# State-space stage: the load of the log/exp table moves from behind the sines to behind the square of B

## The chip, the cores and the metric

One Trainium2 chip, one of its cores. The metric is device time in microseconds (us) of one execution of the whole program; the figure for a kernel is the median of several runs. The engines are TensorE (PE in the profile, its weight loads PEld), VectorE (DVE), ScalarE (ACT), GpSimd (POOL) and SyncE (SP, which issues DMA here).

## The reference

Two layers over x of shape 8 x 512 x 256, float32: causal attention and a sparse SwiGLU, then a selective state space and a mixture of experts. Each is added to its input behind a layer norm. The change is in the state space, of which this is the core (64 heads of 8 channels, state size N = 128):

```python
Bm = (x @ WB.T).reshape(B_, L, H, N)
Cm = (x @ WC.T).reshape(B_, L, H, N)
Bm = rmsnorm(Bm, Bn_w) + B_bias      # x * rsqrt(mean(x*x) + EPS) * w
Cm = rmsnorm(Cm, Cn_w) + C_bias
theta_cumsum = jnp.cumsum(theta * dt[..., None], axis=1)
Bm = rope(Bm, theta_cumsum)          # cos and sin of the summed angles
Cm = rope(Cm, theta_cumsum)
alpha = jnp.exp(dt * A)
h = at * h + bt * outer(B_prev, x_prev) + gt * outer(Bt, xt)   # for each t
yt = einsum(Ct, h)
```

## The kernel before

The program is a row of stages with a barrier behind each. In `state_space` the 64 heads are taken as 32 pairs, and a pair with one of the 8 sequences is a unit: 256 units, one turn of the loop each. The loop is written out for two turns (`j` = 0 and 1) and each engine has its own copy of it, in an order fixed by hand; an engine takes its instructions strictly in that order, and engines meet by semaphores that count turns. There is one buffer of most things, so the engines run as a pipeline over neighbouring turns rather than over copies of a buffer.

TensorE, turn k (`turn`): odd half of B (into `p_b`, waits for the rotation before), angles of the next unit into `p_sum` (waits for `ln_c`), outputs of the unit before the last, even half of B and `b_done`, the exponents of the decays (`e_done`), odd half of C, transposes of the unit before (L1246, L1249: `turned[0]`), the sum of the squares of B over partitions (L1280, waits for GpSimd's `ss_b` and for VectorE's `fr_done`), even half of C (waits for `taken[0]`), more transposes, scores (L1261), chunk sums (L1270), and the sum of the squares of C (L1280 again, waits for GpSimd's `ss_c`). Each projection is six matmuls, lines L48 to L50.

ScalarE, turn k: square of B (L1359, waits for `b_done`, releases GpSimd), exponential of the decays (L1339), a copy that empties the transposes' bank (L1345, `taken[0]`), logarithm and exponential of B's sum (L1350, L1352: together the inverse root), a second copy (L1345), square of C (L1365), logarithm and exponential of C's sum, and then `angles`: Abs (L1330), three sines (L1331, L1332, L1334) of the next unit's angles. Sines need another table than logarithm and exponential, so twice a turn a table is loaded: the sine table, placed by the compiler ahead of the first sine (it stands at L1331), and the log/exp table, asked for at L1335 as the last instruction of `angles`, ahead of the next turn's square.

GpSimd, turn k: adds the two halves of the squares of B (L1159, waits for `sq_b`), finishes C's rotation of the unit before (L1143, L1144), splits a piece of the next pair's weights (L1163, L1165), adds to the decays (L1149, L1150), adds the halves of the squares of C (L1171), scales x (L1180, L1182), finishes B's rotation (L1186, L1187), and builds `own` (L1192).

VectorE, turn k: the phases of the next-but-one angles (`phases`: L1392, the scan L1394, L1396, L1397, which ends with `fr_done`), L1401 and L1402 for the output, normalizing and rotating B (L1409, L1412, L1414, waits for ScalarE's `r_b`), the states (L1419 to L1423), the masked scores (L1428), and normalizing and rotating C (the same lines, waits for `r_c`).

Of the kernel before, what the change touches and what calls it, by code (L numbers as in the profile page):

```python
# [967 lines left out]
def state_space(nc, ctx, w_dram, norm_d, bias_d, left_d, right_d, strict_d, blocks_d, heads_d, tk_dram, dt_dram,  # L968
# [15 lines left out]
    with ExitStack() as mem:  # L984
# [337 lines left out]
        @block.scalar  # L1322
        def _(act):
            A = nc.scalar.activation
            act.wait_ge(const_in, 16 * 7)
            act.wait_ge(const_ready, at_start)

            def angles(count, j):
                act.wait_ge(fr_done, count)
                A(trig[:, j, 1], fr[:], ACT.Abs).then_inc(abs_done, 1)  # L1330
                A(trig[:, j, 0], fr[:], ACT.Sin, scale=UNDER_TURN)  # L1331
                A(trig[:, j, 2], fr[:], ACT.Sin, scale=-UNDER_TURN)  # L1332
                act.wait_ge(abs_done, count)
                A(trig[:, j, 1], trig[:, j, 1], ACT.Sin, bias=quarter[:, 0:1], scale=-UNDER_TURN).then_inc(trig_done, 1)  # L1334
                nc.scalar.preload_act_table_set("natural_log_exp_and_others")  # L1335

            def decays(k):
                act.wait_ge(e_done, k + 1)
                A(dec[:], p_se[:], ACT.Exp).then_inc(d_done, 1)  # L1339

            def take_b(k, j, e):
                act.wait_ge(turned[e], k + 1)
                n = TPB - e
                bank = p_m[:] if e else p_c[:, 0, :]
                A(bt[:, 2 if e else j, 0:n, :], bank[:, 0:n * P].rearrange("p (c t) -> p c t", t=P), ACT.Copy).then_inc(taken[e], 1)  # L1345

            def norms(k, q):
                done, ln, ready = (sum_b, sum_c)[q], (ln_b, ln_c)[q], (r_b, r_c)[q]
                act.wait_ge(done, k + 1)
                A(r[:, q], p_sum[:], ACT.Ln, scale=1.0 / N1, bias=eps[:, 0:1]).then_inc(ln, 1)  # L1350
                act.wait_ge(ln, k + 1)
                A(r[:, q], r[:, q], ACT.Exp, scale=-0.5).then_inc(ready, 1)  # L1352

            angles(1, 0)
            with act.Fori(0, UNITS // 2) as n:
                for j in range(2):
                    k = n * 2 + j
                    act.wait_ge(b_done, k + 1)
                    A(sq[:, 0], p_b[:], ACT.Square).then_inc(sq_b, 1)  # L1359
                    decays(k)  # L1360
                    take_b(k, j, 0)
                    norms(k, 0)
                    take_b(k, j, 1)
                    act.wait_ge(c_done, k + 1)
                    A(sq[:, 1], p_c[:], ACT.Square).then_inc(sq_c, 1)  # L1365
                    norms(k, 1)
                    angles(k + 2, 1 - j)
            decays(UNITS)
            take_b(UNITS, 0, 0)
            take_b(UNITS, 0, 1)  # L1370
# [508 lines left out]
```

## Time and profile before

| | us |
|---|---|
| median of 3 runs | 7745.34 |
| lowest, highest | 7743.88, 7745.35 |
| the profiled execution | 7747.07 |
| its span, first to last instruction | 7745.3 |
| state-space stage in it (2623 to 6985) | 4362 |

The span runs from the first to the last instruction of one profiled execution; its own time is that span and the little that lies around it. In the rows below a time is us from the span's start. A timeline row gives the start, the duration, engine, line, operation, what is written and read, and in brackets how long the engine had been idle and who ended that. PEclk in a view by stretches is TensorE's granted clock as a share of full speed.

### The profile page before, as it was taken

The numbers are of one execution on the slowest core, as the hardware profiler recorded it, in microseconds if no ns is written. First come the engines' busy times: TensorE is split into PE (matmuls) and PEld (weight loads), VectorE is DVE, ScalarE is ACT, GpSimd is POOL, SyncE is SP. The second block draws the span as 40 slices with busy tenths as digits, with TensorE's granted clock in tenths as the row PEclk, the third lists the DMA queues.
The fourth block names the chain that finished last, engine by engine and source line by source line (L and its number), as shares of the span: only waits on it lengthen the run. The fifth ranks groups of instructions, "written<-read, shape, count | busy, mean of one in ns | idle before, by whom it ended". The sixth has DMA issues, their size and how long they took to land. (4 is left out here: it accounts for less than half of the span.)

```text
span 7745.3 us, 137299 instructions
## 1 busy us (share of the span) xinstructions
PE 6985.7 (90%) x43387; PEld 5087.3 (66%) x43660; DVE 4741.5 (61%) x8121; ACT 3713.1 (48%) x5855; POOL 3482.4 (45%) x3893
## 2 busy tenths in 40 slices
PE   6999999999684699999999999999999999997499
PEld 4777777777573566666666666666666666666287
DVE  4333333333555477777777777777777777772433
ACT  2222222222222366666666666666666666662111
POOL 0000000000000477777777777777777777771000
PEclk8555555555796899999999999999999999998699
DMA  1000000000101211111111111111111111112100
GB/s 47 4 9 1 4 9 4 9 4 1 57 22 49 89 27 29 28 27 27 28 29 27 30 27 27 29 27 30 27 28 27 27 29 29 29 27 95 53 22 16
DMA packets 388293, 214.26 MB, mean 28 GB/s; under 512 B 248036, under 2 KB 343076, under 8 KB 387140
## 3 DMA queue, kind: packets, MB, share of 16 engines
q1 hardware_dynamic: 379588, 203.05, 10.1%
q10 hardware_dynamic: 8448, 8.39, 0.3%
q8 instruction: 88, 1.44, 0.1%
q14 instruction: 169, 1.38, 0.1%
HBM read 162.02 MB, written 40.64 MB: 26 GB/s over the span
## 5 line engine op out<-in xcount | busy, mean ns | idle before, releaser
L1117 POOL MEMSET ss_rot<- 128x4096 f32 x1 | 3.5, 3511 | 2500.9 <-POOLq L1815 2500.9
L1350 ACT ACTIVATE ss_r<-ss_pssum,ss_eps 128x512 f32<-128x512 f32 x512 | 352.5, 688 | 1131.1 <-PE ss_pssum L1280 1131.1
L1280 PE MATMUL ss_pssum<-ss_sq,ss_pairssum 128*128 128x512 f32 x1024 | 595.4, 664 | 184.0 <-POOL ss_sq L1171 181.2
L1159 POOL TENSOR_TENSOR ss_sq<-ss_sq 128x512 f32<-128x512 f32 x256 | 329.6, 1288 | 914.9 <-ACT ss_sq L1359 914.9
L1409 DVE SCALAR_TENSOR_TENSOR ss_psb<-ss_psb,ss_norm,ss_r 128x512 f32<-128x512 f32 x512 | 362.9, 755 | 510.3 <-ACT ss_r L1352 510.3
L329 PE MATMUL a_ps_o<-a_probt,a_vhead 128*128 128x128 f32 x2560 | 639.7, 414 | 3.6 <-issue 3.5
L329 PEld LDWEIGHTS a_ps_o<-a_probt,a_vhead 128*128 128x128 f32 x2560 | 604.5, 330 | 4.0 <-ACT a_probt L383 1.6
L1261 PE MATMUL ss_psse<-ss_rot 64*128 64x128 f32 x8224 | 530.0, 279 | 0.3 <-POOL ss_rot L1144 0.3
L427 DVE TENSOR_REDUCE a_nmax<-a_ps_p 128x1 f32<-128x384 f32 (+1 forms) x256 | 159.9, 625 | 598.7 <-PE a_ps_p L305 598.7
L1192 POOL TENSOR_TENSOR ss_own<-ident,ss_tk 128x512 f32<-128x512 f32 x512 | 524.9, 1048 | 0.0
L48 PE MATMUL ss_psb<-x_hi,ss_whi 128*128 x1024 | 515.3, 503 | 6.7 <-DVE ss_fr L1397 4.5
L1261 PEld LDWEIGHTS ss_psse<-ss_rot 64*128 64x128 f32 x8224 | 480.6, 188 | 43.6 <-issue 43.0
L48 PE MATMUL ss_psc<-x_hi,ss_whi 128*128 x1024 | 489.4, 478 | 0.0
L376 ACT ACTIVATE a_prob<-a_ps_p,a_nmax 128x384 f32<-128x384 f32 (+1 forms) x256 | 162.2, 634 | 672.7 <-DVE a_nmax L427 672.6
L1409 DVE SCALAR_TENSOR_TENSOR ss_psc<-ss_psc,ss_norm,ss_r 128x512 f32<-128x512 f32 x512 | 362.7, 754 | 103.7 <-ACT ss_r L1352 103.5
L49 PE MATMUL ss_psb<-x_lo,ss_whi 128*128 x1024 | 408.2, 399 | 0.0
L50 PE MATMUL ss_psb<-x_hi,ss_wlo 128*128 x1024 | 407.7, 398 | 0.0
L50 PE MATMUL ss_psc<-x_hi,ss_wlo 128*128 x1024 | 403.3, 394 | 0.0
L316 PE MATMUL a_ps_t<-ident,a_prob 128*128 128x128 f32 x1280 | 402.6, 438 | 0.1
L49 PE MATMUL ss_psc<-x_lo,ss_whi 128*128 x1024 | 401.1, 392 | 0.0
L1270 PE MATMUL ss_psm<-ss_xe,ss_bt 128*128 128x16 f32 x3084 | 388.6, 264 | 0.0
L1270 PEld LDWEIGHTS ss_psm<-ss_xe,ss_bt 128*128 128x128 f32 x3084 | 363.6, 191 | 31.2 <-issue 0.2
(339 smaller groups left out, 18260.8 us busy)
## 6 DMA issues: line engine op xcount, KB each, us to landing
ss_dtb<-time_steps SPq DMA_DIRECT2D x516, 128.0 KB, 2.9
ss_wraw<-in_w_state SPq DMA_DIRECT2D x264, 80.0 KB, 2.4
ss_xp<-x_heads SPq DMA_DIRECT2D x33, 256.0 KB, 4.4
y_heads<-ss_yo SPq DMA_DIRECT2D x132, 64.0 KB, 2.4
x_heads<-xp_outt SPq DMA_DIRECT2D x32, 256.0 KB, 2.0
ss_right<-decay_rows SPq DMA_DIRECT2D x512, 3.0 KB
ss_left<-decay_rows SPq DMA_DIRECT2D x512, 3.0 KB
op_y<-y_heads SPq DMA_DIRECT2D x8, 1024.0 KB, 6.8
```

Of the source, the lines that this page charges most:

```text
L48: nc.tensor.matmul(out, w_hi, x_hi, start=first, stop=False)
L49: nc.tensor.matmul(out, w_hi, x_lo, start=False, stop=False)
L50: return nc.tensor.matmul(out, w_lo, x_hi, start=False, stop=last)
L316: last = nc.tensor.transpose(p_t[m % 2][:, kt * P:(kt + 1) * P], prob[:, m % PROBS, kt * P:(kt + 1) * P], g.ident[:])
L329: last = nc.tensor.matmul(p_o[half][:, i * P:(i + 1) * P], v_head[:, h % 2, kt, P - DH - at * DH:2 * P - DH - at * DH], probt[:, m % PROBT ...
L1159: G.tensor_tensor(sq[:, 0, 0], sq[:, 0, 0], sq[:, 0, 1], ALU.add).then_inc(ss_b, 1)
L1192: last = G.tensor_tensor(own[:, h * TPB:(h + 1) * TPB], g.ident[:].rearrange("p (o t) -> p o t", o=1).broadcast_to([P, TPB, P]), at_diagon ...
L1261: last = M(p_se[:, h * TPB + c, :], rot[at, 1 - j, e, cols], rot[at, 1 - j, 2 + e, cols], start=e == 0, stop=e == 1)
L1270: last = M(p_m[:, (c * 2 + e) * PW:(c * 2 + e + 1) * PW], bt[:, 2 if e else j, c, :], xe[:, 1 - j, c, :], start=True, stop=True)
L1280: M(p_sum[:], pairs_sum[:], sq[:, q, 0], start=True, stop=True).then_inc((sum_b, sum_c)[q], 1)
L1350: A(r[:, q], p_sum[:], ACT.Ln, scale=1.0 / N1, bias=eps[:, 0:1]).then_inc(ln, 1)
L1409: link.mark(S(bank[:, e, :], bank[:, e, :], norm[:, 2 * q + e:2 * q + e + 1], r[:, q], ALU.mult, ALU.mult))
```

## The change

The call that loads the table of logarithm and exponential is taken out of `angles` and put behind the square of B in the loop. `angles` is also called once before the loop; that load goes too. A load stays in front of the first sine.

```diff
@@ def angles(count, j):
                 act.wait_ge(abs_done, count)
                 A(trig[:, j, 1], trig[:, j, 1], ACT.Sin, bias=quarter[:, 0:1], scale=-UNDER_TURN).then_inc(trig_done, 1)
-                nc.scalar.preload_act_table_set("natural_log_exp_and_others")
 
@@ the loop of ScalarE
                     k = n * 2 + j
                     act.wait_ge(b_done, k + 1)
                     A(sq[:, 0], p_b[:], ACT.Square).then_inc(sq_b, 1)
+                    nc.scalar.preload_act_table_set("natural_log_exp_and_others")
                     decays(k)
                     take_b(k, j, 0)
                     norms(k, 0)
```

## Rows read from the trace of the kernel before

**Rows 1.** The page: span, and busy time by engine (us, share, instructions).

```profile
span 7745.3 us, 137299 instructions
...
PE 6985.7 (90%) x43387; PEld 5087.3 (66%) x43660; DVE 4741.5 (61%) x8121; ACT 3713.1 (48%) x5855; POOL 3482.4 (45%) x3893
```

**Rows 2.** Busy time by stretch: the state-space stage, and one long turn.

```profile
...
core 0: us, PE busy (x) PEld busy (x) DVE busy (x) ACT busy (x) POOL busy (x), PEclk, DMA share, GB/s
2623.00:6985.00 4362.00, 4134.12 (x32440) 2935.62 (x32697) 3401.18 (x4847) 2923.50 (x3832) 3413.46 (x3825) 0.99 0.12 28
4338.28:4356.20 17.92, 16.99 (x126) 12.15 (x126) 13.34 (x20) 11.44 (x15) 13.34 (x15) 0.90 0.08 20
```

**Rows 3.** Line L1359, the square of B: count, duration, first and last start.

```profile
...
L1359 ACT ACTIVATE ss_sq<-ss_psb x256: 1023/1026/1029, 2631.0 to 6984.4; 128x1024 f32<-128x1024 f32 x128
```

**Rows 4.** Waits from 2631 to 6984.4: total us, times, longest.

```profile
...
POOL ss_sq L1159 <- ACT ss_sq L1359: 911.5, 255, 19.1
...
PE ss_pssum L1280 <- POOL ss_sq L1171: 180.4, 252, 0.8
...
ACT ss_sq L1359 <- PE ss_psb L50: 3.7, 2, 3.4
```

**Rows 5.** Timeline of ScalarE in one quiet turn: start us, us, operation, count, idle before.

```profile
...
4424.19 1.03 ACT L1359 ACTIVATE ss_sq<-ss_psb 128x1024 f32<-128x1024 f32 x1
4425.11 1.02 ACT L1339 ACTIVATE ss_dec<-ss_psse 128x1024 f32<-128x1024 f32 x1
4426.76 0.60 ACT L1345 ACTIVATE ss_bt<-ss_psc 128x512 f32<-128x512 f32 x1 [0.62 <-PE ss_psc L1249]
4427.87 0.69 ACT L1350 ACTIVATE ss_r<-ss_pssum,ss_eps 128x512 f32<-128x512 f32 x1 [0.52 <-PE ss_pssum L1280]
...
4434.92 0.69 ACT L1350 ACTIVATE ss_r<-ss_pssum,ss_eps 128x512 f32<-128x512 f32 x1 [3.93 <-PE ss_pssum L1280]
...
4439.16 0.71 ACT L1334 ACTIVATE ss_trig<-ss_trig,ss_quarter 128x512 f32<-128x512 f32 x1
4439.89 1.28 ACT L1335 ACT_TABLE_LOAD   x1
4441.18 1.02 ACT L1359 ACTIVATE ss_sq<-ss_psb 128x1024 f32<-128x1024 f32 x1
```

**Rows 6.** Timeline of GpSimd in the same turn.

```profile
...
4425.30 1.28 POOL L1159 TENSOR_TENSOR ss_sq<-ss_sq 128x512 f32<-128x512 f32 x1 [3.42 <-ACT ss_sq L1359]
...
4432.44 1.26 POOL L1171 TENSOR_TENSOR ss_sq<-ss_sq 128x512 f32<-128x512 f32 x1
```

**Rows 7.** Timeline of TensorE in the same turn.

```profile
...
4426.27 0.42 PE L1249 MATMUL ss_psc<-ss_grown,ss_heads 2*32 2x128 f32 x8
4426.71 1.12 PE L1280 MATMUL ss_pssum<-ss_sq,ss_pairssum 128*128 128x512 f32 x2
4427.40 0.66 PE L48 MATMUL ss_psc<-x_hi,ss_whi 128*128 x1
...
4433.75 1.12 PE L1280 MATMUL ss_pssum<-ss_sq,ss_pairssum 128*128 128x512 f32 x2 [0.79 <-POOL ss_sq L1171]
...
4439.93 0.39 PE L50 MATMUL ss_psb<-x_hi,ss_wlo 128*128 x1
```

**Rows 8.** Timeline of VectorE in the same turn and into the next.

```profile
...
4425.73 0.69 DVE L1397 SCALAR_TENSOR_TENSOR ss_fr<-ss_fr,ss_pssum 128x512 f32<-128x512 f32 x1
...
4429.25 1.42 DVE L1409 SCALAR_TENSOR_TENSOR ss_psb<-ss_psb,ss_norm,ss_r 128x512 f32<-128x512 f32 x2 [2.09 <-ACT ss_r L1352]
...
4434.65 1.22 DVE L1428 TENSOR_TENSOR ss_gm<-ss_psse,ss_dec 128x1024 f32<-128x1024 f32 x1
4436.30 1.42 DVE L1409 SCALAR_TENSOR_TENSOR ss_psc<-ss_psc,ss_norm,ss_r 128x512 f32<-128x512 f32 x2 [0.43 <-ACT ss_r L1352]
...
4442.82 0.69 DVE L1397 SCALAR_TENSOR_TENSOR ss_fr<-ss_fr,ss_pssum 128x512 f32<-128x512 f32 x1
```

**Rows 9.** Timeline of TensorE in the long turn of rows 2.

```profile
...
4347.83 2.07 PE L1280 MATMUL ss_pssum<-ss_sq,ss_pairssum 128*128 128x512 f32 x2 [0.77 <-POOL ss_sq L1171]
```

## The prediction

> **What bounds the kernel now.** I read the page first: one span of 7745.3 us in which TensorE is busy 90%, so the first guess is that nothing on ScalarE matters [rows 1]. The view by stretches corrects it. The state-space stage (2623 to 6985 us) is 56% of the span, and in it TensorE is busy 4134 of 4362 us, ScalarE and GpSimd far less [rows 2]. It runs 256 turns, from the first square of B at 2631.0 to the last at 6984.4 [rows 3], 4353.4 us for 255 turns, 17.07 us each. The reader is to see in the view of waits that the largest idle time of TensorE proper, 180.4 us in 252 waits (0.72 each), stands ahead of the matmul L1280 that sums the squares of C, and that GpSimd's L1171 ends it [rows 4]. Neither of those engines is the cause: both are links of a ring.
>
> The timeline of one quiet turn shows the ring with every link tight. ScalarE squares B at 4424.19, done at 4425.22 [rows 5]. GpSimd has waited for that alone: L1159 starts at 4425.30 and its queue then runs without a gap of over 0.2 us until L1171 ends at 4433.70 [rows 6]. TensorE, idle for 0.79, takes L1280 at 4433.75, done at 4434.87 [rows 7]. ScalarE takes the logarithm at 4434.92, then the exponential, Abs, a load of the sine table, three sines until 4439.87, the load of the log/exp table at L1335 from 4439.89 to 4441.17, and the next square of B at 4441.18 [rows 5]. 4441.18 - 4424.19 = 16.99 us. The load removed from this place is 1.28 us of that ring, less what becomes late next. The square's input is complete when the last L50 of B ends, 4439.93 + 0.39 = 4440.32 [rows 7]; so the square now waits 0.86 us for a table which it doesn't need.
>
> **Part by part.** *Removed:* the load behind the sines, 1.28 us, 256 times, plus one before the loop. The latter costs nothing either way: ScalarE idles 3.4 us before the first square [rows 4]. *Added:* the same load behind the square, 256 times. After the last turn the loop now leaves the sine table, so one load must come before the last exponential L1339, where there was one before it too: 0. No wait or semaphore is added, no DMA issue moves, no operation of another engine changes.
>
> *The square.* With the load gone ScalarE is free at 4439.87, before 4440.32. Add 0.05 from a matmul's end to ScalarE's start (4434.87 to 4434.92): the square starts at 4440.37, 0.81 us earlier.
>
> *What queues behind the moved load.* The exponential of the decays L1339, the copy L1345, then the logarithm of B. From the sines' end through the load to the square is 1.31 us [rows 5]. So: square 4440.37 to 4441.40, load to 4442.70, exponential to 4443.72, and the copy can start from 4443.63 (one starts 0.09 before the last ends). In the turn shown the exponential ended at 4426.13 and the copy waited 0.62 for TensorE's L1249, to 4426.76 [rows 5]; one turn on that is 4443.75. The cover is 0.62, the delay 0.50: the load is hidden with 0.12 to spare. GpSimd, which adds to the decays at L1149, comes to them only behind four other operations. If the cover fails, each microsecond of it beyond some 0.2 pushes the copy, and with it the matmuls of C that wait for the bank it empties.
>
> For the price of a load the trace and the Trainium skill disagree. Here 1.31 us lie between the end of the last sine and the square's start, of which 1.28 are the load and 0.03 is everything else [rows 5]. The Trainium skill (ScalarE: Activation LUTs, "What ACT_TABLE_LOAD costs") gives the load the same 1283 ns, but adds about 1380 ns of drain, 2.66 us for each switch. By that the copy would start at about 4444.99 and the change would lose (the third rival). The trace speaks against it twice a turn, both times behind an activation into SBUF; none in this stage stands behind one that reads PSUM, as the square does.
>
> *What is late next.* The gain isn't 0.81 for sure: three rings close just below 16.99.
> - ScalarE/GpSimd/TensorE, the old one with the square waiting for its matmuls: L1280 at 4433.75 to 4440.32 is 6.57; 0.05; square's start to L1171's end 9.51 (4424.19 to 4433.70); 0.05. Sum 16.18 us.
> - TensorE's own order without its idle time: 16.99 - 0.79 = 16.20 us [rows 7]; with the mean wait of 0.72, 16.27.
> - VectorE's. From the start of C's normalizing L1409 (4436.30) to the end of the next turn's phases L1397 (4442.82 + 0.69 = 4443.51) its queue is full: 7.21. From L1409 for B (4429.25) to L1428's end (4435.87), less the overlap of 0.09, it is full too: 6.53. Between them the phases release L1280 for B, whose start to the logarithm's is 1.16 (4426.71 to 4427.87), and on to VectorE's start 1.38 (to 4429.25): 2.54 [rows 5, 7, 8]. The lag from VectorE to TensorE is the unknown: now 0.29 lies between 4426.42 and 4426.71, but TensorE was busy with L1249 until 4426.69. By the nearest rows it is 0.05 (GpSimd to TensorE) or, as an upper end, the 0.29. So 7.21 + 6.53 + 2.54 + 0.05 to 0.29 = 16.33 to 16.57 us. I take 0.08, near the low end, since the 0.05 are a wait that truly ended so and the 0.29 are covered: 16.36.
>
> VectorE's ring is the longest, and it decides: 16.99 - 16.36 = 0.63 us a quiet turn, 255 turns, 161 us. The idle of 0.43 before C's L1409 [rows 8] shows where it comes from: that slack and the lag before L1280 are all the ring has.
>
> **The clock.** Not all turns are quiet: 4353.4 - 255 x 16.99 = 21 us are extra. One such turn is 17.92 us long with a granted clock of 0.90 [rows 2]; in it the summing matmuls took 2.07 us against 1.12 right after an idle time of 0.77 [rows 9], so TensorE was at the lower of its two levels (1.2 against 2.4 GHz). At 0.93 each the 21 us are 22 or 23 such turns. The change takes most of that idle time away, so the falls should not become more; I count half of them gone, 10 us. Bounds: all gone, 21 us saved; a fall in every fifth turn, 51 x 0.93 = 47, which is 26 lost.
>
> The execution profiled took 7747.07 us around its span of 7745.3. 7747.07 - 161 - 10 = 7576; the median of the plain runs lies 1.7 below the profiled one, so 7574.
>
> **Rivals.**
> 1. *The square needs a table of its own.* Sines leave their table active; if Square isn't in it, a load is put ahead of the square again and a second follows. For it: every square of B in the trace runs under the log/exp table. Against: Abs and the copies never had a load of their own beside either table. Price: the old ring of 16.99 stays. The copy starts 0.69 later than now (1.31 less the cover of 0.62) and ends so much nearer to what TensorE needs: L1280 keeps it until 4427.83, 0.43 after the copy has let it go (4427.40), so it loses 0.26 of its 0.79 of slack [rows 7]. The logarithm, now 0.51 behind the copy's end, is 0.18 late, and VectorE's ring stays under 16.8. No change: 7745. The Trainium skill (ScalarE: Activation LUTs, "Table sets: the hidden batching unit") says cheap functions are in every set, and doesn't name Square among its examples.
> 2. *VectorE's ring doesn't bind*, its gaps inside the queue shrinking. Then TensorE's 16.20 holds: 0.79 x 255 + 10 = 211, 7534.
> 3. *Slower: the load behind the square costs twice.* Place: between L1359 and L1339. At 2 x 1.31 = 2.62 the copy starts at 4444.94, 1.19 later than now (4443.75). TensorE loses 1.19 - 0.43 = 0.76, its order becomes 16.96; the logarithm of B is 1.19 - 0.51 = 0.68 late and adds that to VectorE's 16.36: 17.04 [rows 5, 7]. It decides from about 2.57 us: above it, slower. At 2.62: +0.05 x 255 = 13, 7758; at 3 us 0.43 a turn, 7855. Against it stand both loads of each turn. By the skill's 2.66 the same sum gives 17.08, some 23 us slower.
> 4. *The clock falls far more often*, because turns of another length meet it elsewhere. Half of the turns: 128 x 0.93 = 119 against 161 + 21: 7682. For it: the fall shown comes at one place of the turn. Against: that place is the idle time that goes.
>
> **How the numbers follow.** Forecast 0.82; rival 1 0.05; rival 2 0.05; rival 3 0.03; rival 4 0.05. The likeliest case gives 7574. Its bounds: with VectorE's ring at 16.57 and the falls kept, 0.42 x 255 = 107, 7637; with TensorE's ring and all falls gone 7523. A measurement tells from no change what is over about 0.2% (15 us). The range 7530 to 7620 takes in rival 2 and most of the lag's bounds, and leaves out rivals 1, 3 and 4 and the far end of the lag. Faster by over 0.2%: forecast, rivals 2 and 4, 0.92. Within: rival 1 and a rival 3 that just decides, 0.06. Slower 0.02.
>
> **What would show it.** Squares of B 16.3 to 16.4 us apart; before them ScalarE waits for the last L50, some 0.3 to 0.5 us, where it waited for nothing. The load stands directly behind the square, 1.28 us, with no wait before it and none before the decays. The copy's wait of 0.62 falls to about 0.1. TensorE's 180 us ahead of L1280 shrink to under 50, and it waits for VectorE's L1397 instead; VectorE's 0.43 before C's L1409 is gone. I am wrong if that idle stays, if loads stand at L1359, if the copy starts over 0.4 us late against L1249's end, or if the granted clock of the stage is below 0.98.

## The result, and the profile after

7559.48 us (median of 4 runs, 7558.90 to 7561.97) against 7745.35: a ratio of 0.9761, 95% interval 0.9744 to 0.9778. The profiled execution took 7559.73 us, its span is 7557.9. A second set of 5 runs gave 7560.08 and 0.9757. In the changed kernel the square of B is line L1358, the moved load L1359, the exponential of the decays L1338, the copy L1344 and the logarithm L1349; the other engines' lines are the same.

The page after, its span and busy time by engine:

```profile
span 7557.9 us, 137572 instructions
...
PE 6957.1 (92%) x43660; PEld 5057.0 (67%) x43660; DVE 4717.7 (62%) x8121; ACT 3739.7 (49%) x5855; POOL 3485.0 (46%) x3893
```

The view by stretches, the state-space stage (columns as in [rows 2]):

```profile
...
2623.00:6800.00 4177.00, 4104.29 (x32717) 2906.17 (x32718) 3380.36 (x4851) 2952.32 (x3835) 3420.48 (x3830) 1.00 0.12 29
```

The square of B, its count and its first and last start (against [rows 3]):

```profile
...
L1358 ACT ACTIVATE ss_sq<-ss_psb x256: 1023/1023/1024, 2631.0 to 6794.5; 128x1024 f32<-128x1024 f32 x128
```

The first square stands at the same 2631.0 and the last at 6794.5: 4163.5 us for 255 turns, 16.33 each against 17.07. From first to last square the stage is 189.9 us shorter, the span 187.4; what lies behind the last square took 763.4 us against 760.9. In the fourteen traces of this document that stretch takes 760.9 to 765.6 us, with no order by kernel, so the 2.5 us are within its scatter. The waits of the stage (against [rows 4]):

```profile
...
POOL ss_sq L1159 <- ACT ss_sq L1358: 722.3, 256, 19.2
...
ACT ss_sq L1358 <- PE ss_psb L50: 111.9, 256, 4.8
...
PE ss_pssum L1280 <- DVE ss_fr L1397: 71.0, 244, 0.3
```

The 180.4 us ahead of L1280 that GpSimd's L1171 ended are gone. TensorE now waits for VectorE's L1397, 71.0 us, and ScalarE waits for the matmuls of B, 111.9 us, where it hardly ever had. One turn of ScalarE (against [rows 5]):

```profile
...
4344.89 1.02 ACT L1358 ACTIVATE ss_sq<-ss_psb 128x1024 f32<-128x1024 f32 x1 [0.41 <-PE ss_psb L50]
4345.93 1.28 ACT L1359 ACT_TABLE_LOAD   x1
4347.22 1.02 ACT L1338 ACTIVATE ss_dec<-ss_psse 128x1024 f32<-128x1024 f32 x1
4348.37 0.60 ACT L1344 ACTIVATE ss_bt<-ss_psc 128x512 f32<-128x512 f32 x1
4349.76 0.69 ACT L1349 ACTIVATE ss_r<-ss_pssum,ss_eps 128x512 f32<-128x512 f32 x1 [0.79 <-PE ss_pssum L1280]
...
4360.10 0.71 ACT L1334 ACTIVATE ss_trig<-ss_trig,ss_quarter 128x512 f32<-128x512 f32 x1
4361.21 1.02 ACT L1358 ACTIVATE ss_sq<-ss_psb 128x1024 f32<-128x1024 f32 x1 [0.41 <-PE ss_psb L50]
```

The square waits 0.41 us for the last L50. The load follows 0.02 behind it, 1.28 long, and the exponential 0.01 behind that, ending at 4348.24; the copy starts at 4348.37, 0.13 later. So the load is under cover, and the copy has 0.13 us to spare before it is late. TensorE in the same turn (against [rows 7]):

```profile
...
4347.88 0.42 PE L1249 MATMUL ss_psc<-ss_grown,ss_heads 2*32 2x128 f32 x8
4348.60 1.12 PE L1280 MATMUL ss_pssum<-ss_sq,ss_pairssum 128*128 128x512 f32 x2 [0.29 <-DVE ss_fr L1397]
...
4353.35 1.51 PE L1270 MATMUL ss_psm<-ss_xe,ss_bt 128*128 128x16 f32 x12
4354.71 1.10 PE L1280 MATMUL ss_pssum<-ss_sq,ss_pairssum 128*128 128x512 f32 x2
```

The second L1280, the one of C, follows L1270 with no idle time, where 0.79 had been. The first, the one of B, now stands 0.30 behind L1249. VectorE (against [rows 8]) shows why:

```profile
...
4347.85 0.69 DVE L1397 SCALAR_TENSOR_TENSOR ss_fr<-ss_fr,ss_pssum 128x512 f32<-128x512 f32 x1
...
4351.15 1.42 DVE L1409 SCALAR_TENSOR_TENSOR ss_psb<-ss_psb,ss_norm,ss_r 128x512 f32<-128x512 f32 x2 [1.87 <-ACT ss_r L1351]
...
4356.54 1.22 DVE L1428 TENSOR_TENSOR ss_gm<-ss_psse,ss_dec 128x1024 f32<-128x1024 f32 x1
4357.68 1.41 DVE L1409 SCALAR_TENSOR_TENSOR ss_psc<-ss_psc,ss_norm,ss_r 128x512 f32<-128x512 f32 x2
```

L1397 ends at 4348.54 and L1280 starts at 4348.60, a lag of 0.06; L1428 runs straight into C's L1409, whose wait of 0.43 is gone. VectorE's ring is closed: each of its links now starts as soon as the one before it lets it.

### The profile page after: what moved, and what is told of

Its sections match the earlier page's. It is cut to its first block and busy times, and to the rows that moved or that the text cites. A ratio compares the mean times of both kernels' runs of the same rounds, so it can differ in the third digit from the quotient of the medians.

```text
span 7557.9 us, 137572 instructions
## 1 busy us (share of the span) xinstructions
PE 6957.1 (92%) x43660; PEld 5057.0 (67%) x43660; DVE 4717.7 (62%) x8121; ACT 3739.7 (49%) x5855; POOL 3485.0 (46%) x3893
## 5 line engine op out<-in xcount | busy, mean ns | idle before, releaser
L1349 ACT ACTIVATE ss_r<-ss_pssum,ss_eps 128x512 f32<-128x512 f32 x512 | 352.3, 688 | 962.1 <-PE ss_pssum L1280 962.1
L1409 DVE SCALAR_TENSOR_TENSOR ss_psb<-ss_psb,ss_norm,ss_r 128x512 f32<-128x512 f32 x512 | 362.7, 754 | 447.8 <-ACT ss_r L1351 447.8
L1280 PE MATMUL ss_pssum<-ss_sq,ss_pairssum 128*128 128x512 f32 x1024 | 570.9, 639 | 72.4 <-DVE ss_fr L1397 71.3
L48 PE MATMUL ss_psc<-x_hi,ss_whi 128*128 x1024 | 532.2, 520 | 0.0
L1261 PE MATMUL ss_psse<-ss_rot 64*128 64x128 f32 x8224 | 530.0, 279 | 1.2 <-POOL ss_rot L1144 1.2
L48 PE MATMUL ss_psb<-x_hi,ss_whi 128*128 x1024 | 518.6, 506 | 4.5 <-DVE ss_fr L1397 4.5
L1261 PEld LDWEIGHTS ss_psse<-ss_rot 64*128 64x128 f32 x8224 | 480.6, 188 | 44.4 <-issue 42.9
L50 PE MATMUL ss_psc<-x_hi,ss_wlo 128*128 x1024 | 403.3, 394 | 0.0
L50 PE MATMUL ss_psb<-x_hi,ss_wlo 128*128 x1024 | 403.2, 394 | 0.0
L1270 PE MATMUL ss_psm<-ss_xe,ss_bt 128*128 128x16 f32 x3084 | 389.7, 265 | 0.0
L1270 PEld LDWEIGHTS ss_psm<-ss_xe,ss_bt 128*128 128x128 f32 x3084 | 364.7, 192 | 31.2 <-issue 0.2
L427 DVE TENSOR_REDUCE a_nmax<-a_ps_s 128x1 f32<-128x128 f32 (+1 forms) x256 | 91.5, 358 | 450.4 <-PE a_ps_s L305 450.3
```

The lines of the kernel that those rows point to most:

```text
L48: nc.tensor.matmul(out, w_hi, x_hi, start=first, stop=False)
L50: return nc.tensor.matmul(out, w_lo, x_hi, start=False, stop=last)
L1261: last = M(p_se[:, h * TPB + c, :], rot[at, 1 - j, e, cols], rot[at, 1 - j, 2 + e, cols], start=e == 0, stop=e == 1)
L1270: last = M(p_m[:, (c * 2 + e) * PW:(c * 2 + e + 1) * PW], bt[:, 2 if e else j, c, :], xe[:, 1 - j, c, :], start=True, stop=True)
L1280: M(p_sum[:], pairs_sum[:], sq[:, q, 0], start=True, stop=True).then_inc((sum_b, sum_c)[q], 1)
L1409: link.mark(S(bank[:, e, :], bank[:, e, :], norm[:, 2 * q + e:2 * q + e + 1], r[:, q], ALU.mult, ALU.mult))
```

## The experiments

The time of a turn is that from the first to the last square of B in the trace, over 255. Ratios are to the kernel before on the same chip.

| run | change | us | ratio (95%) | us a turn |
|---|---|---|---|---|
| before | | 7745.4 to 7751.6 | 1 | 17.07 |
| after | | 7559.5 | 0.9761 (0.9744 to 0.9778) | 16.33 |
| before_short_sine | before, L1332 cut | 7627.1 | 0.9841 (0.9824 to 0.9857) | 16.62 |
| after_short_sine | after, L1332 cut | 7560.7 | 0.9755 (0.9739 to 0.9771) | 16.33 |
| after_two_loads | one more load | 7723.9 | 0.9967 (0.9955 to 0.9980) | 16.95 |
| after_no_loads | no sines | 7561.5 | 0.9757 (0.9741 to 0.9774) | 16.33 |
| before_short_phases | before, without L1396 | 7748.5 | 0.9998 (0.9988 to 1.0007) | 17.06 |
| after_short_phases | after, without L1396 | 7509.5 | 0.9691 (0.9675 to 0.9707) | 16.13 |
| after_long_phases | after, L1396 twice | 7744.5 | 0.9993 (0.9984 to 1.0003) | 17.05 |
| before_long_phases | before, L1396 twice | 7746.3 | 0.9995 (0.9986 to 1.0005) | 17.06 |
| after_phases_sbuf | after, scan into SBUF | 7745.3 | 0.9997 (0.9988 to 1.0006) | 17.06 |
| after_states | after, sums in SBUF | 7988.9 | 1.0313 (1.0299 to 1.0327) | 17.96 |
| after_again | the changed kernel | 7560.1 | 0.9757 (0.9744 to 0.9771) | 16.33 |
| after_states_psum | after, without L1421 | 7522.2 | 0.9703 (0.9690 to 0.9717) | 16.17 |

**Is it ScalarE's ring before, and no longer after?** One of three sines made short, in both kernels:

```diff
-                A(trig[:, j, 2], fr[:], ACT.Sin, scale=-UNDER_TURN)
+                A(trig[:, j, 2, 0:8], fr[:, 0:8], ACT.Sin, scale=-UNDER_TURN)
```

> The kernel before with the sine at L1332 cut from 512 columns to 8 (most of the third table is left at zero, so the angles' part of the rotation is left out). Of the 0.62 us some 0.42 should go, by the slope between the copies of 384 and 512 columns. Theory (before the change the ring over ScalarE, GpSimd and TensorE sets the turn, 16.99 us): everything between C's logarithm and B's square counts in full, so 16.99 - 0.42 = 16.57 us a turn, about 7640 us. Rival (the load was special, other ScalarE time is hidden): 16.99, 7745. TensorE's idle time ahead of L1280 for C falls from 0.72 to about 0.3, and the granted clock falls less often than 22 times.

> The same cut sine in the changed kernel. Theory (VectorE's ring of 16.33 us sets the turn now, ScalarE waits for the matmuls of B): nothing moves, 16.33 us a turn, 7559 us; ScalarE's wait before B's square grows by 0.42. Rival (ScalarE's time still counts, the ring is only shorter): 16.33 - 0.42 = 15.9, about 7452.

The sine takes 0.19 us in place of 0.62. Both runs went as the theory had it: before, the usual turn is 16.58 us (16.62 with the long ones), 0.41 less than 16.99; after, nothing moves. In the kernel before, TensorE's wait for GpSimd shrinks to 96.5 us, 0.41 each (about 0.3 was expected), and the clock falls 6 times where it fell 22 times. In the changed one ScalarE's wait for the matmuls grows from 0.44 us a turn to 0.84. The first fence is from the waits of the first run, the second from those of the second run, both from 2640 to 6790.

```profile
...
PE ss_pssum L1280 <- POOL ss_sq L1171: 96.5, 234, 0.5
```

```profile
...
ACT ss_sq L1358 <- PE ss_psb L50: 214.1, 254, 1.0
```

**How much cover has the load?**

```diff
                     A(sq[:, 0], p_b[:], ACT.Square).then_inc(sq_b, 1)
+                    nc.scalar.preload_act_table_set("gelu_and_others")
                     nc.scalar.preload_act_table_set("natural_log_exp_and_others")
```

> The changed kernel with one more table load (another set, which nothing uses) ahead of the log/exp load behind the square. Theory (the load is hidden only as far as the copy L1344 waits for TensorE): the copy now has 0.1 us to spare, so it starts 1.1 us later, the matmuls of C wait for the bank, and from B's square through two loads, the exponential and the copy (5.2 us) and TensorE's own order to the next end of B (11.7 us) the ring is 16.95 to 17.0 us, about 7720 us. Rival (time behind the square costs nothing): 16.33, 7559. Rival (each load on ScalarE costs its 1.28 in full): 17.6, 7885.

16.95 us and 7723.9, as the theory had it: the ring through the copy. TensorE waits for the copy ahead of the L48 of C's even half, 87.7 us in the stage, and ScalarE's square still waits for TensorE. ScalarE's timeline of that run:

```profile
...
4412.92 1.02 ACT L1358 ACTIVATE ss_sq<-ss_psb 128x1024 f32<-128x1024 f32 x1 [0.38 <-PE ss_psb L50]
4413.96 1.28 ACT L1359 ACT_TABLE_LOAD   x1
4415.25 1.28 ACT L1360 ACT_TABLE_LOAD   x1
4416.54 1.02 ACT L1338 ACTIVATE ss_dec<-ss_psse 128x1024 f32<-128x1024 f32 x1
4417.46 0.59 ACT L1344 ACTIVATE ss_bt<-ss_psc 128x512 f32<-128x512 f32 x1
```

The second load costs 16.95 - 16.33 = 0.62 us a turn of its 1.28, and takes back 0.0206 of the 0.0239 that the change gave in the ratio. The other 0.66 us are free. The ring through the copy is 16.95 with two loads, so it is 15.67 with one, well under VectorE's 16.33. That is more room than the 0.13 us by which the copy is early, since TensorE does B's L1280 before it needs the bank that the copy empties. This is the third rival's mechanism, met with a second load of 1.28 us in place of a load that costs twice. Its price was put at 17.04 and is 16.95.

**Does either load still cost?** Squares in place of the three sines:

```diff
-                A(trig[:, j, 0], fr[:], ACT.Sin, scale=UNDER_TURN)
-                A(trig[:, j, 2], fr[:], ACT.Sin, scale=-UNDER_TURN)
+                A(trig[:, j, 0], fr[:], ACT.Square, scale=UNDER_TURN)
+                A(trig[:, j, 2], fr[:], ACT.Square, scale=-UNDER_TURN)
 (and the third in the same way)
```

> The changed kernel with the three sines computed as squares instead (the rotation's values are left out), so that no table is loaded in the loop but the one that is asked for, and that only where the compiler keeps it. Theory: both loads are hidden now, so the turn stays at 16.33 us, 7559 us. Rival (the sine table's load of 1.28 ahead of the sines still costs): up to 1.3 us a turn less, near 15.1 to 16.2 us, under 7530.

16.33, as expected. The load at L1331 is gone in all turns; that behind the square stayed, and the compiler put one ahead of the square (L1358) in every second turn, so this run has 1.5 loads a turn and not one. It shows that the load ahead of the sines costs nothing; that the load behind the square costs nothing is shown by the run above, where 0.66 us of a further load were free. ScalarE waits longer for the matmuls of B, 303.2 us where it was 111.9:

```profile
...
ACT ss_sq L1358 <- PE ss_psb L50: 303.2, 254, 1.9
```

**Is VectorE the next ring?** Its phases made shorter, and longer, in both kernels:

```diff
-                link(V.tensor_scalar(fr[:], p_sum[:], MAGIC, None, ALU.add))
-                V.scalar_tensor_tensor(fr[:], fr[:], MAGIC, p_sum[:], ALU.subtract, ALU.subtract).then_inc(fr_done, 1)
+                V.scalar_tensor_tensor(fr[:], p_sum[:], 0.0, ones[:], ALU.mult, ALU.mult).then_inc(fr_done, 1)
 (short; long is the first of the two lines written twice)
```

> The kernel before with one of VectorE's phase steps left out (the rounding L1396, 0.69 us and its wait; the angles are set to zero, so the rotation's values are left out). Theory: before the change VectorE's ring (16.33) is not the one that binds, so the turn stays at 16.99 us, 7745. If VectorE's time counted there, 16.3 and under 7600.

> The same step left out of the changed kernel. Theory: VectorE's ring falls to about 15.6 us and the next ones bind, TensorE's own order at 16.20 to 16.27 and the ScalarE, GpSimd and TensorE ring at 16.18: 16.2 to 16.27 us a turn, 7527 to 7545, and TensorE's wait ahead of B's L1280 for VectorE goes. Rival (TensorE already binds at 16.33): 16.33, 7559. Rival (VectorE alone binds, nothing close behind it): 15.6, about 7375.

> The changed kernel with the phase step L1396 done twice (0.72 us more in VectorE's queue, the same result). Theory: VectorE binds, so all of it counts: 16.33 + 0.72 = 17.05 us a turn, about 7743. Rival (TensorE binds, VectorE has room): under 16.6, below 7630. TensorE then idles some 0.7 us ahead of B's L1280 in place of C's; whether the granted clock falls there as it did before the change tells if it is the idle time as such or its place next to the small matmuls of L1270: falls in about one turn of twelve cost 0.08 more a turn.

> The same doubled step in the kernel before. Theory: VectorE had 16.99 - 16.33 = 0.66 us to spare there, so of 0.72 only 0.06 counts: 17.05 us a turn, some 15 us, 7745 to 7765. Rival (the step counts in full in either kernel): 17.7, about 7930. Beside the run above it: if both kernels take the same 17.05, the moved load is worth nothing once VectorE is the longer ring.

Before the change 0.72 us less in VectorE's queue is worth nothing; after it, 0.20 us a turn and 50 us, until the next ring at 16.13. The square of B in the shortened one:

```profile
...
L1358 ACT ACTIVATE ss_sq<-ss_psb x256: 1023/1023/1024, 2629.2 to 6743.2; 128x1024 f32<-128x1024 f32 x128
```

(6743.2 - 2629.2) / 255 = 16.13. What binds there is the old ring again, with the square waiting for its matmuls. GpSimd's L1171 ends at 4348.84, and C's L1280 starts 0.05 behind it, as it did before the change:

```profile
...
4347.57 1.27 POOL L1171 TENSOR_TENSOR ss_sq<-ss_sq 128x512 f32<-128x512 f32 x1
```

```profile
...
4347.43 1.51 PE L1270 MATMUL ss_psm<-ss_xe,ss_bt 128*128 128x16 f32 x12
4348.89 1.12 PE L1280 MATMUL ss_pssum<-ss_sq,ss_pairssum 128*128 128x512 f32 x2
```

From L1270's start to L1280's it is 1.46 us here and 1.36 (4353.35 to 4354.71) in the changed kernel, where L1280 waits for nothing. So TensorE's own order is 0.10 shorter still, 16.03.

With 0.72 us more in VectorE's queue, both kernels take 17.05 to 17.06 us: with VectorE's ring that long, the place of the load is worth nothing. The wait ahead of B's L1280 in the changed kernel with the long phases, and its granted clock:

```profile
...
PE ss_pssum L1280 <- DVE ss_fr L1398: 259.2, 254, 1.0
```

```profile
...
2640.00:6970.00 4330.00, 4029.12 (x32242) 2884.95 (x32492) 3538.95 (x5079) 2931.12 (x3807) 3421.36 (x3809) 1.00 0.12 28
```

**Can VectorE's ring be shortened with the same result?** Three tries. The first lets TensorE go on after the scan:

```diff
-                link(V.tensor_tensor_scan(p_sum[:], ones[:], p_sum[:], 0.0, ALU.mult, ALU.add))
+                V.tensor_tensor_scan(ph[:], ones[:], p_sum[:], 0.0, ALU.mult, ALU.add).then_inc(scanned, 1)
+                dve.wait_ge(scanned, count)
 (L1396 and L1397 read ph, and TensorE waits for scanned in place of fr_done)
```

> The changed kernel, with VectorE's scan of the phases written into an SBUF tile instead of back into the PSUM bank, so that TensorE's L1280 for B waits for the scan (a semaphore of its own) and no longer for the two steps behind it (L1396, L1397); the result is the same. Theory: VectorE's ring loses the two steps, 1.44 us, since they then fall into its idle time before the inverse root of B; it goes to 14.9 us and no longer binds. TensorE's full order and the ScalarE ring, 16.07 to 16.13 us in the run with the shortened phases, bind: 16.1 us a turn, 7500 to 7512 us. Rival (VectorE's queue as a whole is what binds, wherever its work stands): 16.33, 7559. Rival (without a wait for VectorE the order falls below 16.0): under 7490.

None of the three was met: 17.06 us. VectorE's wait did leave the path, but L1398 and L1399 (the former L1396 and L1397), which now read SBUF alone, got longer, and GpSimd's L1144 and L1145 beside them too. VectorE's timeline of that run, then GpSimd's, its wait of TensorE, and the stretch:

```profile
...
4418.59 0.94 DVE L1398 TENSOR_SCALAR ss_fr<-ss_ph 128x512 f32<-128x512 f32 x1
4419.57 1.64 DVE L1399 SCALAR_TENSOR_TENSOR ss_fr<-ss_fr,ss_ph 128x512 f32<-128x512 f32 x1
```

```profile
...
4419.21 1.45 POOL L1144 TENSOR_TENSOR ss_rot<-ss_rot,ss_tmp 128x512 f32<-128x512 f32 x1
4420.62 1.74 POOL L1145 TENSOR_TENSOR ss_rot<-ss_rot,ss_tmp 128x512 f32<-128x512 f32 x1
```

```profile
...
PE ss_pssum L1281 <- POOL ss_sq L1172: 143.3, 253, 0.7
```

```profile
...
2640.00:6970.00 4330.00, 4184.84 (x32500) 2941.73 (x32499) 3667.43 (x4822) 2931.37 (x3808) 3552.14 (x3806) 0.98 0.12 28
```

0.69 and 0.69 became 0.94 and 1.64 us, and 1.27 and 1.26 became 1.45 and 1.74. The cause is GpSimd beside them and not SBUF as such: the first two times, at the start of the stage, GpSimd is idle beside them, and the same two operations take 0.43 and 0.69 us.

```profile
...
2627.09 0.43 DVE L1398 TENSOR_SCALAR ss_fr<-ss_ph 128x512 f32<-128x512 f32 x1
2627.55 0.69 DVE L1399 SCALAR_TENSOR_TENSOR ss_fr<-ss_fr,ss_ph 128x512 f32<-128x512 f32 x1
```

Over the stage GpSimd's two grow by 0.61 us a turn in the mean, and its sums for C are late by that. So C's L1280 waits again (143.3 us), the usual turn is 16.73 us (16.13 and 0.61 are 16.74), and on top of it the clock fell 51 times. The second try takes the copy out of the chain of states, but through SBUF:

```diff
-                link(V.tensor_tensor(sums, sums, blocks[:]..., ALU.mult))
-                link(V.tensor_copy(entering(1), added[:, 0]))
-                link(S(entering(2), entering(1), ends[:, ds(at + 1, 1)], added[:, 1], ALU.mult, ALU.add))
+                link.mark(V.tensor_tensor(own_sums[:], sums, blocks[:]..., ALU.mult))
+                link.wait()
+                link.mark(S(entering(2), into[:, 0], first, into[:, 1], ALU.mult, ALU.add))
+                link.mark(V.tensor_copy(entering(1), into[:, 0]))
+                link.wait()
 (into is own_sums by groups; the third S reads it too)
```

> The changed kernel, with the masked chunk sums (L1419) written to SBUF, and the first state's copy (L1421) taken out of the chain of states: VectorE reads the two registers once and the copy overlaps; the result is the same. Of VectorE's 16.33 us ring 0.1 to 0.25 us should go (the copy is 0.19, with one link of waiting). Theory: each bit of it counts until 16.13 is reached: 16.1 to 16.25 a turn, 7510 to 7540. Rival (only the phases are on the path): 16.33, 7559.

Wrong by far: 17.96 us. VectorE's timeline, then GpSimd's:

```profile
...
4523.82 0.59 DVE L1424 SCALAR_TENSOR_TENSOR ss_state<-ss_ownsums,ss_ends 128x32 f32<-128x32 f32 x1 [0.60 <-DVE ss_ownsums L1419]
4524.34 1.32 DVE L1425 COPY ss_state<-ss_ownsums 128x32 f32<-128x32 f32 x1
4525.81 0.86 DVE L1427 SCALAR_TENSOR_TENSOR ss_state<-ss_state,ss_ends,ss_ownsums 128x32 f32<-128x32 f32 x1
```

```profile
...
4523.08 1.28 POOL L1186 TENSOR_TENSOR ss_rot<-ss_rot,ss_tmp 128x512 f32<-128x512 f32 x1
4524.32 1.30 POOL L1187 TENSOR_TENSOR ss_rot<-ss_rot,ss_tmp 128x512 f32<-128x512 f32 x1
```

The same 32 columns that took 0.25, 0.19 and 0.25 us with an operand in PSUM (the lines L1422, L1421, L1423 of the changed kernel) take 0.59, 1.32 and 0.86; the first two end at 4524.41 and 4525.66, 0.04 to 0.05 after GpSimd's L1186 (4524.36) and L1187 (4525.62). GpSimd keeps its 1.28 and 1.30. Over the whole stage the three take 0.54, 0.98 and 0.93 us in the mean, 1.76 more a turn than in the changed kernel, and the turn is 1.63 longer. The new order of the three with operands in PSUM wasn't run by itself. The third try keeps an operand of each operation in PSUM:

```diff
-                link(V.tensor_tensor(sums, sums, blocks[:]..., ALU.mult))
-                link(V.tensor_copy(entering(1), added[:, 0]))
+                link.mark(V.tensor_tensor(entering(1), sums[:, 0:2], mask(2), ALU.mult))
+                link(V.tensor_tensor(sums[:, 2:6], sums[:, 2:6], mask(4), ALU.mult))
```

> The changed kernel, with the copy L1421 dropped: the first group of the masked chunk sums is written by its own masking operation straight into the state, the other two stay in PSUM as before; every VectorE operation keeps one operand in PSUM; the result is the same. One operation of 0.19 us and one wait between dependent operations leave VectorE's ring, one short operation comes in, net 0.1 to 0.2 us. Theory (VectorE's ring binds at 16.33, and the run with state sums in SBUF was slow by the longer operations on SBUF operands, 0.98 and 0.93 us, not by the new order): 16.13 to 16.23 us a turn, 7510 to 7535 us, with GpSimd's operations at their 1.28. Rival (a shorter chain of states cannot help): 16.33, 7560.

16.17 us, as expected, and 7522.2 us: 0.9703, clear of the 0.9757 of the changed kernel (0.9744 to 0.9771). Its square, and the wait that had been 71.0 us:

```profile
...
L1358 ACT ACTIVATE ss_sq<-ss_psb x256: 1023/1023/1024, 2629.0 to 6753.0; 128x1024 f32<-128x1024 f32 x128
```

```profile
...
PE ss_pssum L1280 <- DVE ss_fr L1397: 7.3, 47, 0.2
```

## Why the prediction was right, and where it was not

- *The ring and its release.* Right. In the kernel before, 0.41 us less ScalarE time gave 0.41, and 0.72 less VectorE time gave nothing.
- *The square, 0.81 us earlier, then waiting for its matmuls.* Right: 0.41 of wait in the turn shown, 0.3 to 0.5 forecast.
- *The cover.* Right, and as thin as put: 0.13 us left against 0.12. The load behind an activation that reads PSUM costs 1.28 and 0.03 around it. The Trainium skill's 2.66 us for a switch (ScalarE: Activation LUTs, "What ACT_TABLE_LOAD costs") isn't met here. Two loads take 2.60 from the square's end (4413.94) to the exponential's start (4416.54); that run shows what nearly 2.66 would have left: 0.33% of the time. One detail was miscounted: GpSimd comes to L1149 behind five operations, not four; nothing hangs on it.
- *What is late next: VectorE at 16.36.* Right: 16.33, the lag being 0.06 where 0.08 was taken. The next rings were put too high. ScalarE's, put at 16.18, is 16.13 by the run with the short phases; TensorE's own order, put at 16.20 to 16.27, is 16.03.
- *The clock.* This term was mis-sized: half of the 21 us were counted as saved, all were. In the trace after, no fall is recorded in the stage and the granted clock is 1.00. That is 11 of the 14.5 us between 7574 and 7559.5; the 0.03 us of the ring are 8 more. The other way go 2.5 us of scatter behind the stage and 1.5 in the step from the profiled execution to the median, which was taken as 1.7 and is 0.3. The sum is 15.
- *TensorE's wait ahead of L1280.* Forecast under 50 us in sum, measured 71.0, all for L1397. A ring of 16.36 over TensorE's 16.20 leaves 41 us, so the bound went with its terms; it is TensorE's own order that was too long. With the 16.33 and 16.03 that the runs show it is 76, near the 71.0.
- *The rivals.* No load was added ahead of the square, so the first falls. (The prediction's sign "loads at L1359" means the square's line in the kernel before. In the changed kernel the square is L1358 and has no load; the L1359 there is the moved load itself.) The second fell too, since VectorE does bind. The third's condition isn't met, and its sum was too high: two loads gave 16.95, which is its term for TensorE (16.96, in part by luck, since it started from an order 0.17 too long), and not the 17.04 of VectorE; the logarithm of B started 1.28 behind L1280's start in place of 1.16, 0.12 late and not 0.68. So even a load of twice the price would have left the kernel a little faster. The fourth had the sign wrong. The outer bound 7637 is 7638 by its own terms.

## What to carry to other kernels

An instruction of an idle-looking engine is worth its whole length when it stands on a closed ring; follow the timeline from one release to the next until it comes back to its start, and add up the other rings as well, since the second longest is all that the change can win. Work that must be done is best put behind the release of the next engine, where its cover can be read as the wait of the next instruction: here 0.62 us of cover, 0.50 used. The wait of the next instruction is the least of the room: by the run with two loads some 0.66 us more would have been free. When a ring is shortened by taking an operand out of PSUM, look first at what the other engine on SBUF does at that moment.

## What the runs showed of the hardware

VectorE and GpSimd slow each other when VectorE's operation has no operand in PSUM. A copy of 128x32 from SBUF took 0.98 us in the mean and 1.32 in the turn shown, against 0.19 from PSUM. VectorE's 128x512 step of two SBUF operands took 1.64 us with GpSimd running and 0.69 with GpSimd idle, while GpSimd's operation beside it grew from 1.26 to 1.74. With one operand in PSUM there is no such effect: L1396 and L1397 of the changed kernel take 0.69 us in every turn, with GpSimd running or idle. The Trainium skill (SBUF — State Buffer, "Who interferes with whom") says that a VectorE instruction with two SBUF inputs contends with a GpSimd instruction that reads SBUF, and that in VectorE's two-port modes, which a copy can enter, whichever engine issues first holds the shared pair of ports for its whole instruction and the other is blocked. The copies agree: in all 256 turns the copy ends 0.03 to 0.14 us behind the end of GpSimd's L1186 or L1187. The growth on both sides in the run with the scan in SBUF agrees with the first half of that; which of them held the ports when, no row shows.

The falls of TensorE's clock hang on where it idles, more than on how long. Counted in the trace's record of the granted clock in the stage: 22 in the kernel before, 17 (`before_short_phases`) and 51 (`after_phases_sbuf`) in two others where C's L1280 waits 0.6 to 0.8 us behind the small matmuls L1270, and 6 where it waits 0.4. Every one of them is recorded between 0.1 us ahead of the start of a C's L1280 and 1.8 us behind it. The shorter wait of 0.6 has more falls than that of 0.8. There are none in the three kernels (the two with the long phases, and the sums in SBUF) where TensorE idles 1.0 us a turn ahead of B's L1280. That place has small matmuls in front of it too, but few: 0.8 us of transposes (L1246, L1249) and ahead of them the projection of C, where C's L1280 has 3.9 us of L1246, L1261 and L1270. The cause isn't settled, since the length of the turn differs as well.
